# Attention and mixture-of-experts layer on one core: first layers three experts ahead, two bank sets, and the routing weights prepared in two parts

## The chip, the cores and the metric

The kernel runs on one core of one Trainium2 chip, as one launch. The metric is the device time of an execution in microseconds (us); a kernel's time is the median of its runs. Engines: PE is TensorE (PEld its weight loads), DVE is VectorE, ACT is ScalarE, POOL is GpSimd, SP is SyncE, which here only issues transfers.

## The reference

`x` has shape (16, 512, 128) in float32. Two sub-layers follow each other, each added to its input:

```python
x = x + attention(layernorm(x))      # 16 heads of 8, softmax over 512, relative keys and values
n = layernorm(x)                     # second sub-layer, per token
shared = (gelu(n @ sw1 + sb1) @ sw2 + sb2).sum(experts) / 2          # 2 shared experts
gates = n @ router_w + router_b                                      # 8 experts
topv, topi = top_k(gates, 2); probs = softmax(topv)
comb = sum_k one_hot(topi) * probs                                   # (tokens, 8)
y = gelu(n @ w1 + b1) @ w2 + b2                                      # all 8 experts, hidden width 256
x = x + shared + (comb * y).sum(experts)
```

All ten experts are computed for every token; `comb` weighs their results.

## The kernel before

The first 1612 us are attention, in 8 pairs of batches. The change lies in the part behind it, the experts' part: 16 batches of 512 tokens, each with ten experts (two shared, eight routed). The tokens of a batch lie on the free axis of `h_hi` and `h_lo`, the float16 high and low halves of the normalised rows, so a float32 product is made of three float16 ones.

**One expert.** PE's `up` makes the first layer: two halves of the hidden width, each three matmuls with 512 columns, into banks 4 and 5 of PSUM. ACT's `hidden` takes each half through the gelu into `hid` (two instructions, L692), then copies both to float16, `hid_h` (L698). POOL's `low_rows` subtracts (L545): `hid_l = hid - hid_h`, both operands and the result in SBUF. PE's `down` makes the second layer: 24 matmuls with 128 columns, into bank 6 for even experts and bank 7 for odd ones. DVE's `expert` adds the result into `acc`, weighed by `comb` (four instructions, L1025), and raises `y_used`. In the trace `hid` is called probs, `hid_h` and `hid_l` are called probs_t, and `acc`, `h_hi` and `h_lo` are called keys, since they lie in those buffers.

**The order on PE** is written out by hand in `batch`. With LOOK = 2, the step of expert e issues `up(e + 2)` and then `down(e)`; the last two steps issue the first layers of the next batch's experts 0 and 1. Between the steps the next batch is prepared: attention's remainder after step 0 (`prepare_attention`), the output projection after step 1, the transposes of the normalised rows after step 4 (`prepare_h`), the gates after step 5. The routing weights of the batch itself are transposed after step 0 (`prepare_comb`), and after step 2 they are multiplied with the second biases (`second_biases`). These use banks 0 to 3.

**What `down` waits for.** It needs `hid_l` of its expert, and its bank must be free: for experts 2 to 9 that `y_used` of expert e - 2 has come, for experts 0 and 1 that the last expert of the batch before is added (`final_ready`). So `down(9)` waits for DVE to have added expert 7.

**The next batch on DVE.** DVE works in program order: after expert 1 it makes the residual and the statistics, after expert 4 `h_lo`, after expert 5 the gates, the two best of the eight (`gap` is the difference of the two) and `pick`, their one-hot rows. POOL raises e to the power `gap` (`gate_exponentials`, L539, after its subtraction for expert 7), and DVE makes the softmax of two and the weighted `pick`, after expert 7 (L1004 to L1012).

**Loops.** Batches 0 to 13 run in a hardware loop of 7 iterations with two batches each; batches 14 and 15 are written out behind it. Each iteration begins with a load of ACT's function table.

Of the kernel before, what the change touches and what calls it, by code (L numbers as in the profile page):

```python
# [17 lines left out]
P = 128  # L18
# [43 lines left out]
LOOK = 2  # L62
# [12 lines left out]
OWN = {(0, 1): "values0", (1, 0): "values1"}  # L75

# [9 lines left out]
def attention_ffn(nc, x, w_qkv, cols, rows, wo_t, bo, rk_win, rv_win, rw, rb, w1, w2, b2,  # L86
                  sw1, sw2, sb2, b1_cols, consts, rel_scratch, out):
    with ExitStack() as ctx:
# [106 lines left out]
        comb_t = sb("comb_t", [EXPERTS, L])  # L195
# [6 lines left out]
        hid = probs[:, 0:4, :].rearrange("p (e k) c -> p e k c", e=2)  # L202
# [39 lines left out]
        SETUP_POOL = 4  # L242
# [181 lines left out]
        def _(pool):  # L424
# [3 lines left out]
            nc.gpsimd.memset(comb[:], 1.0 / NS / W_SCALE).then_inc(setup_pool, 1)  # L428
            pool.wait_ge(setup_pool, SETUP_POOL)
# [111 lines left out]
            def low_rows(b, slot, e):  # L541

                pool.wait_ge(hid_high, START + b * EXPERTS + e + 1)
                n = slot * EXPERTS + e
                nc.gpsimd.tensor_tensor(hid_l[:, n % SLOTS, :, :], hid[:, n % 2, :, :], hid_h[:, n % SLOTS, :, :],  # L545
                                        ALU.subtract).then_inc(hid_low, 1)
# [19 lines left out]
        def _(act):  # L566
# [118 lines left out]
            def hidden(b, slot, e):  # L685
                n = slot * EXPERTS + e

                act.wait_ge(hid_low, SLOTS + b * EXPERTS + e - 1)
                for k in range(2):

                    act.wait_ge(up_done, START + b * 20 + e * 2 + k + 1)
                    nc.scalar.activation(hid[:, n % 2, k, :], ps[:, 4 + k, :], ACT.Gelu, bias=b1_s[:, e, k:k + 1],  # L692
# [5 lines left out]
                nc.scalar.activation(hid_h[:, n % SLOTS, :, :], hid[:, n % 2, :, :], ACT.Copy).then_inc(hid_high, 1)  # L698

            def batch(b, slot, ahead):  # L700
                for e in range(EXPERTS):
                    hidden(b, slot, e)
                    if e == 2:
                        prepare_weights(b)
                    if ahead and e == 5:
                        normalised(b + 1, 1 - slot)
                    if ahead and e == 6:
                        prepare_h(b + 1, 1 - slot)

            def prepare_weights(b):  # L710

                act.wait_ge(comb_tr, START + b + 1)
                nc.scalar.activation(comb_t[:], ps[0:EXPERTS, 2, :], ACT.Copy).then_inc(comb_t_ready, 1)
# [34 lines left out]
        def _(dve):  # L748
# [164 lines left out]
            def last_step(pair, parity):  # L913
# [16 lines left out]
                rel_out(pair, s)  # L930
                prepare_comb(0, 0, link)
# [12 lines left out]
            FFN_LINKS = 14  # L944
# [36 lines left out]
            def prepare_gates(b, link):  # L981

                dve.wait_ge(gate_done, START + b + 1)
                link(nc.vector.tensor_tensor(gates[:], ps[:, 2, 0:TPB * NE].rearrange("p (t e) -> p t e", t=TPB),
# [16 lines left out]
            def prepare_comb(b, slot, link):  # L1001
# [8 lines left out]
                link(nc.vector.tensor_tensor(pick[:], pick[:], prob2[:].unsqueeze(3).broadcast_to([P, TPB, 2, NE]), ALU.mult))  # L1010
                link.wait()
                nc.vector.tensor_tensor(comb[:, slot, :, NS:], pick[:, :, 0, :], pick[:, :, 1, :], ALU.add).then_inc(comb_ready, 1)  # L1012

            def second_biases(b, slot):

                dve.wait_ge(bias_done, START + b + 1)
                nc.vector.tensor_tensor(acc[:, slot, :, :], ps[:, 3, :].rearrange("p (t d) -> p t d", t=TPB),
                                        acc[:, slot, :, :], ALU.add).then_inc(bias_added, 1)
# [75 lines left out]
            nc.vector.tensor_scalar(b2_s[:], b2_s[:], W_SCALE, None, ALU.mult).then_inc(w_low, 1)  # L1094
# [10 lines left out]
        def _(pe):  # L1105
# [276 lines left out]

            def prepare_attention(b, parity, pair):
# [5 lines left out]


                pe.wait_ge(x1_var, START + b)
# [20 lines left out]
            def prepare_gates(b, slot):  # L1412

                pe.wait_ge(h_ready, START + 2 * b + 1)
                for t in range(TPB):
                    last = nc.tensor.matmul(ps[:, 2, t * NE:(t + 1) * NE], h_t[:, slot, t * P:(t + 1) * P], rw_s[:], start=True, stop=True)
# [9 lines left out]
            def second_biases(b):  # L1426

                pe.wait_ge(comb_t_ready, START + b + 1)
# [155 lines left out]
```

## Time and profile before

| what | value |
|---|---|
| median of 3 runs | 2149.46 us (2146.33 to 2150.55) |
| the profiled execution's own time | 2150.59 us |
| its span, first to last instruction | 2147.1 us |
| PE busy | 2082.1 us, 97% of the span |
| DVE, ACT, POOL busy | 76%, 70%, 54% of the span |
| PE's share of the chain that ended last | 84% |
| TensorE's granted clock over the span | 0.992 |

The span leaves out some 3.5 us around the first and the last instruction. The profiled execution is 1.1 us above the median. In rows of the timeline a matmul's duration is longer than the distance to the next one, since matmuls overlap: what an instruction costs PE is the distance between starts.

### The profile page before, as it was taken

What the parts mean: (1) busy time and instruction counts of PE and PEld (TensorE: products, weight loads), DVE (VectorE), ACT (ScalarE), POOL (GpSimd) and SP (SyncE); (2) the same over time, 40 slices, a digit from 0 to 9 for tenths busy, and PEclk for the clock granted to TensorE, in tenths of its full rate; (3) what the DMA queues carried; (4) which work ended last, traced back from release to release, by engine and by line L of the source; (5) the groups of instructions that cost most, each with busy time, mean ns of one, the idle gap of its engine ahead of it and who ended that gap; (6) DMA issues with size and microseconds to landing.
All of it is one profiled execution on the core that took longest, in us unless ns stands there. A gap on an engine that the chain in (4) does not pass through costs nothing.

```text
span 2147.1 us, 88171 instructions
## 1 busy us (share of the span) xinstructions
PE 2082.1 (97%) x37442; PEld 1544.8 (72%) x37442; DVE 1637.8 (76%) x3856; ACT 1513.3 (70%) x3304; POOL 1161.0 (54%) x1104
## 2 busy tenths in 40 slices
PE   3999999999999999999999999999998999999998
PEld 1777777777777777777777777777775777777776
DVE  4787787788778878977887787788875676677675
ACT  3666676666676676767666776766656888888887
POOL 5454546356354644544563455454415677777676
PEclk8999999999999999999999999999999999999999
DMA  5112211321221123123112211222112212212210
GB/s 139 33 55 66 74 55 45 86 65 54 62 79 55 45 66 81 49 59 89 48 53 66 75 55 55 76 62 58 44 55 23 30 20 24 29 20 24 29 20 11
DMA packets 255681, 114.48 MB, mean 53 GB/s; under 512 B 142218, under 2 KB 251156, under 8 KB 255348
## 3 DMA queue, kind: packets, MB, share of 16 engines
q1 hardware_dynamic: 255348, 109.60, 21.0%
q8 instruction: 263, 4.31, 0.8%
q14 instruction: 70, 0.57, 0.1%
HBM read 83.34 MB, written 8.39 MB: 43 GB/s over the span
## 4 chain that ended last, share of the span: by engine, by line
PE 84%; ACT 5%; POOL 4%; issue 3%; SPq 1%; DVE 1%; DMA 1%; ACTq 0%; POOLq 0%; DVEq 0%
PE ps L1276 21%; PE ps L1211 11%; PE ps L1296 10%; PE ps L1306 8%; PE ps L1218 8%; PE ps L1229 7%; POOL probs_t L545 3%; ACT probs L692 2%; PE ps L1458 2%; PE ps L1441 2%; PE ps L1443 2%; PE ps L1442 2%; PE ps L1460 2%; PE ps L1459 2%; PE ps L1314 1%
## 5 line engine op out<-in xcount | busy, mean ns | idle before, releaser
L624 ACT ACTIVATE probs<-ps,neg_max 128x512 f32<-128x512 f32 x1024 | 690.5, 686 | 352.2 <-DVE neg_max L819 352.1
L819 DVE TENSOR_REDUCE neg_max<-ps 128x1 f32<-128x512 f32 x1024 | 635.5, 682 | 151.7 <-PE ps L1218 147.3
L463 POOL TENSOR_TENSOR stat_hi<-q_twice,mask8h 128x1024 f16<-128x1024 f16 x128 | 242.8, 1897 | 659.1 <-PE ps L1218 594.2
L1276 PE MATMUL ps<-const,probs 128*128 128x128 f32 x4096 | 496.4, 274 | 0.7 <-ACT probs L624 0.6
L1276 PEld LDWEIGHTS ps<-const,probs 128*128 128x128 f32 x4096 | 453.4, 141 | 28.9 <-issue 15.5
L824 DVE COPY probs_t<-ps 128x512 f32<-128x512 f32 x512 | 339.5, 683 | 92.1 <-PE ps L1276 89.4
L545 POOL TENSOR_TENSOR probs_t<-probs,probs_t 128x1024 f16<-128x1024 f32 x160 | 340.1, 2134 | 108.8 <-ACT probs_t L698 108.8
L614 ACT ACTIVATE probs_t<-ps 128x512 f32<-128x512 f32 x512 | 278.6, 595 | 135.9 <-PE ps L1276 133.5
L1211 PE MATMUL ps<-keys,stat_hi 128*32 128x512 f16 x4096 | 318.0, 383 | 0.0
L1218 PE MATMUL ps<-rk_split,stat_rel 96*32 96x512 f16 (+2 forms) x4096 | 281.4, 340 | 0.0
L1025 DVE SCALAR_TENSOR_TENSOR keys<-ps,comb,keys 128x128 f32<-128x128 f32 x640 | 179.7, 343 | 128.7 <-PE ps L1460 128.6
L479 POOL TENSOR_TENSOR stat_rel<-q_rel,mask4h 96x1024 f16<-96x1024 f16 x128 | 251.1, 1962 | 41.7 <-PE ps L1218 30.2
L692 ACT ACTIVATE probs<-ps,b_s 128x512 f32<-128x512 f32 x320 | 205.4, 684 | 53.9 <-PE ps L1443 48.9
L1306 PE MATMUL ps<-probs_t,rv_step 128*32 128x128 f32 x6656 | 226.5, 273 | 2.4 <-DMA rv_step<-in_rv_win 2.4
L1458 PE MATMUL ps<-w_h,probs_t 128*128 128x128 f16 x1280 | 222.8, 219 | 5.3 <-DVE keys L1025 1.8
L1296 PE MATMUL ps<-probs_t,v_s 128*32 128x128 f32 x6656 | 226.2, 272 | 0.0
L1460 PE MATMUL ps<-w_h,probs_t 128*128 128x128 f16 x1280 | 222.6, 219 | 0.0
L1459 PE MATMUL ps<-w_l,probs_t 128*128 128x128 f16 x1280 | 222.6, 219 | 0.0
L624 ACT ACTIVATION_READ_ACCUMULATOR probs<-ps,neg_max 128x1 f32 x1024 | 207.4, 203 | 0.0
L1211 PEld LDWEIGHTS ps<-keys,stat_hi 128*32 128x32 f16 x4096 | 91.3, 96 | 158.1 <-issue 108.2
L1296 PEld LDWEIGHTS ps<-probs_t,v_s 128*32 128x32 f32 x6656 | 185.2, 109 | 22.1 <-issue 0.3
L473 POOL TENSOR_TENSOR stat_lo<-q_lo_pair,mask8h 128x128 f16<-128x128 f16 x512 | 191.2, 406 | 0.0
(135 smaller groups left out, 2900.4 us busy)
## 6 DMA issues: line engine op xcount, KB each, us to landing
rv_step<-in_rv_win SPq DMA_DIRECT2D x128, 512.0 KB, 3.9
keys<-keys SPq DMA_DIRECT2D x64, 96.0 KB, 2.7
x_pair<-in_x SPq DMA_DIRECT2D x8, 512.0 KB, 4.6
q_twice<-q_hi SPq DMA_DIRECT2D x32, 128.0 KB, 2.9
q_lo_pair<-q_lo SPq DMA_DIRECT2D x32, 128.0 KB, 2.6
rel_scratch<-rel_t SPq DMA_DIRECT2D x256, 16.0 KB, 3.2
x_pair<-in_x SPq DMA_DIRECT2D x16, 256.0 KB, 3.1
x_pair<-rel_scratch SPq DMA_DIRECT2D x64, 64.0 KB, 3.9
```

The costliest lines, as they stand in the source:

```text
L545: nc.gpsimd.tensor_tensor(hid_l[:, n % SLOTS, :, :], hid[:, n % 2, :, :], hid_h[:, n % SLOTS, :, :], ALU.subtract).then_inc(hid_low, 1)
L614: nc.scalar.activation(probs_t[s % 2][:, q, :, :].rearrange("p r c -> p (r c)"), ps[:, tr_bank(q), :], ACT.Copy).then_inc(evac_act, 1)
L624: nc.scalar.activation(probs[:, q, :], ps[:, i, :], ACT.Exp, bias=neg_max[:, q:q + 1], accum_out=row_sum[parity][:, s * QUADS + q:s * QUAD ...
L819: nc.vector.tensor_reduce(neg_max[:, q:q + 1], ps[:, i, :], op=ALU.max, axis=AX_X, negate=True).then_inc(max_done, 1)
L824: nc.vector.tensor_copy(probs_t[s % 2][:, q, :, :].rearrange("p r c -> p (r c)"), ps[:, tr_bank(q), :]).then_inc(evac_dve, 1)
L1211: nc.tensor.matmul(ps[at:at + 32, q % IN_ROUND, :], stat_hi[s % 2][:, half, b, q, :], group_keys(k_both[parity][:, half, b, :], group), st ...
L1218: last = nc.tensor.matmul(ps[32 * g:32 * g + 32, q % IN_ROUND, L - near:L], stat_rel[s % 2][:, q, g, :, :].rearrange("k l h -> k (l h)"), ...
L1276: last = nc.tensor.transpose(ps[:, bank, rt * P:(rt + 1) * P], probs[:, q, rt * P:(rt + 1) * P], ident)
L1296: nc.tensor.matmul(ps[32 * g:32 * g + 32, AV_BANK, b * P:(b + 1) * P], values[:, 32 * g:32 * g + 32], cols, start=rt == 0, stop=rt == RT - ...
L1306: last = nc.tensor.matmul(ps[32 * g:32 * g + 32, AV_BANK, (2 + half) * P:(3 + half) * P], rv_step[:, RT - 1 - block, q * 32:q * 32 + 32], ...
L1458: nc.tensor.matmul(y, hid_h[:, place, k, rows], w2_h[:, e, k, :], start=k == 0, stop=False)
L1459: nc.tensor.matmul(y, hid_h[:, place, k, rows], w2_l[:, e, k, :], start=False, stop=False)
```

## The change

LOOK becomes 3: a step issues `up(e + 3)` and `down(e)`. First layers of even experts go to banks 4 and 5, those of odd ones to banks 2 and 3 (`up_bank`), and `up` waits for the gelu of the expert two before. `hid` has four places in place of two. All preparation now uses banks 0 and 1. The routing weights are split into float16 parts on DVE (`comb_split`: high, low, high) before PE transposes them, and the second biases too (`b2_split`), so that their product is one float16 matmul per 128 tokens over 96 rows. That product moves to after step 3, the transposes to after step 1. `down(0)` waits for expert 8 of the batch before in place of expert 9. POOL's two powers come later in its order, and DVE's softmax part stands alone as `prepare_choice`, after expert 6.

```diff
-LOOK = 2
+LOOK = 3
+def up_bank(e, k):
+    return (4 if e % 2 == 0 else 2) + k
...
-        hid = probs[:, 0:4, :].rearrange("p (e k) c -> p e k c", e=2)
+        hid = probs[:].rearrange("p (e k) c -> p e k c", e=SLOTS)
...
             def batch(b, slot, ahead):            # POOL
                 for e in range(EXPERTS):
                     low_rows(b, slot, e)
-                    if ahead and e == 3:
+                    if ahead and e == 5:
                         deviations_after(b + 1)
-                    if ahead and e == 7:
+                    if ahead and e == 8:
                         gate_exponentials(b + 1)
...
             def hidden(b, slot, e):               # ACT
-                act.wait_ge(hid_low, SLOTS + b * EXPERTS + e - 1)
+                act.wait_ge(hid_low, SLOTS + b * EXPERTS + e - SLOTS + 1)
...
-                    if e == 2:
+                    if e == 4:
                         prepare_weights(b)
-                    if ahead and e == 5:
+                    if ahead and e == 6:
                         normalised(b + 1, 1 - slot)
-                    if ahead and e == 6:
+                    if ahead and e == 7:
                         prepare_h(b + 1, 1 - slot)
...
-            def prepare_comb(b, slot, link):      # DVE
+            def prepare_choice(b, link):
...
                 link(nc.vector.tensor_tensor(pick[:], pick[:], prob2[:].unsqueeze(3).broadcast_to([P, TPB, 2, NE]), ALU.mult))
+
+            def prepare_comb(b, slot, link):
+
                 link.wait()
-                nc.vector.tensor_tensor(comb[:, slot, :, NS:], pick[:, :, 0, :], pick[:, :, 1, :], ALU.add).then_inc(comb_ready, 1)
+                link(nc.vector.tensor_tensor(comb[:, slot, :, NS:], pick[:, :, 0, :], pick[:, :, 1, :], ALU.add))
+                link.wait()
+
+                dve.wait_ge(comb_tr, START + b)
+                weights = comb[:, slot, :, :]
+                link(nc.vector.tensor_scalar(comb_split[:, :, 0:3:2, 0:EXPERTS], weights.unsqueeze(2).broadcast_to([P, TPB, 2, EXPERTS]),
+                                             W_SCALE, None, ALU.mult))
+                link.wait()
+                nc.vector.scalar_tensor_tensor(comb_split[:, :, 1, 0:EXPERTS], weights, W_SCALE, comb_split[:, :, 0, 0:EXPERTS],
+                                               ALU.mult, ALU.subtract).then_inc(comb_ready, 1)
...
+                        if e == 6:
+                            prepare_choice(b + 1, link)
                         if e == 7:
                             prepare_comb(b + 1, 1 - slot, link)
...
-                    last = nc.tensor.transpose(ps[0:EXPERTS, 2, t * P:(t + 1) * P], comb[:, slot, t, :], ident)
+                    halves_of = comb_split[:, t, :, :].rearrange("p a e -> p (a e)")
+                    last = nc.tensor.transpose(bank_h(0, L)[0:3 * 32, t * P:(t + 1) * P], halves_of, identh[:])
...
-                    last = nc.tensor.matmul(ps[:, 3, t * D:(t + 1) * D], comb_t[:, t * P:(t + 1) * P], b2_s[:], start=True, stop=True)
+                    last = nc.tensor.matmul(ps[:, 1, t * D:(t + 1) * D], comb_t[:, t * P:(t + 1) * P], b2_split[:], start=True, stop=True)
...
-                    pe.wait_ge(gelu_done, START + b * 20 + (e * 2 + k - 1 if e else 0))
+                    if b is not first_batch or e >= 2:
+
+                        pe.wait_ge(gelu_done, START + b * 20 + e * 2 + k - 3)
...
-                if e >= 2:
-                    pe.wait_ge(y_used, START + b * (EXPERTS - 1) + e - 1)
+                if e == 1:
+                    pe.wait_ge(final_ready, START + b)
                 else:
-                    pe.wait_ge(final_ready, START + b)
+                    pe.wait_ge(y_used, START + b * (EXPERTS - 1) + max(e - 1, 0))
...
-                    if e == 0:
+                    if e == 1:
                         prepare_comb(b, slot)
-                    if e == 2:
-                        second_biases(b)
+                    if e == 3:
+                        second_biases(b, ahead)
```

On DVE, in batch 14, where the code is written out, these rows stand between the one-hot rows of the next batch and the second biases. The row of keys<-ps,comb,keys is `expert`, four instructions for each expert, so x8 are experts 6 and 7. In the kernel before:

```order
L996 TENSOR_TENSOR gap<-top 128x4
L998 TENSOR_TENSOR pick<-const,top_f 128x64
L1025 SCALAR_TENSOR_TENSOR keys<-ps,comb,keys 128x128 x8
L1004 TENSOR_SCALAR prob<-e_gap 128x4
L1006 RECIPROCAL prob<-prob 128x4
L1008 TENSOR_TENSOR prob<-prob,e_gap 128x4
L1010 TENSOR_TENSOR pick<-pick,prob 128x64
L1012 TENSOR_TENSOR comb<-pick 128x4x8
```

And in the changed kernel, at the same place:

```order
L1008 TENSOR_TENSOR gap<-top 128x4
L1010 TENSOR_TENSOR pick<-const,top_f 128x64
L1049 SCALAR_TENSOR_TENSOR keys<-ps,comb,keys 128x128 x4
L1016 TENSOR_SCALAR prob<-e_gap 128x4
L1018 RECIPROCAL prob<-prob 128x4
L1020 TENSOR_TENSOR prob<-prob,e_gap 128x4
L1022 TENSOR_TENSOR pick<-pick,prob 128x64
L1049 SCALAR_TENSOR_TENSOR keys<-ps,comb,keys 128x128 x4
L1027 TENSOR_TENSOR comb<-pick 128x4x8
L1032 TENSOR_SCALAR comb_split<-comb 128x4x2x10
L1035 SCALAR_TENSOR_TENSOR comb_split<-comb,comb_split 128x4x10
```

Four of the five steps of the softmax part now stand ahead of expert 7, and two new instructions follow the fifth.

On POOL, in the same batch, the row of probs_t is the subtraction for one expert. In the kernel before:

```order
L545 TENSOR_TENSOR probs_t<-probs,probs_t 128x1024 [waits hid_high] x4
L532 TENSOR_TENSOR rstd<-var_eps,half_pow 128x4 [waits x1_var]
L534 TENSOR_TENSOR shift<-neg_mean,rstd 128x4 [waits pool_link]
L545 TENSOR_TENSOR probs_t<-probs,probs_t 128x1024 [waits hid_high] x4
L539 TENSOR_TENSOR e_gap<-e_const,gap 128x4 [waits gap_ready]
L545 TENSOR_TENSOR probs_t<-probs,probs_t 128x1024 [waits hid_high] x12
```

And in the changed kernel:

```order
L555 TENSOR_TENSOR probs_t<-probs,probs_t 128x1024 [waits hid_high] x6
L542 TENSOR_TENSOR rstd<-var_eps,half_pow 128x4 [waits x1_var]
L544 TENSOR_TENSOR shift<-neg_mean,rstd 128x4 [waits pool_link]
L555 TENSOR_TENSOR probs_t<-probs,probs_t 128x1024 [waits hid_high] x3
L549 TENSOR_TENSOR e_gap<-e_const,gap 128x4 [waits gap_ready]
L555 TENSOR_TENSOR probs_t<-probs,probs_t 128x1024 [waits hid_high] x11
```

The first power moved behind two more subtractions, the second behind one more. Behind the second, the rest of the batch's experts and all of batch 15 follow.

## Rows read from the trace of the kernel before

**Rows 1.** The page's first part: busy us, share of the span and instructions.
```profile
PE 2082.1 (97%) x37442; PEld 1544.8 (72%) x37442; DVE 1637.8 (76%) x3856; ACT 1513.3 (70%) x3304; POOL 1161.0 (54%) x1104
```

**Rows 2.** Timeline of ACT: start us, us, engine, line, operation, tiles, count, idle before.
```profile
1689.50 1.28 ACT L692 ACT_TABLE_LOAD   x1 [0.85 <-POOL probs_t L545]
...
1754.18 1.28 ACT L692 ACT_TABLE_LOAD   x1 [0.85 <-POOL probs_t L545]
...
1767.80 1.34 ACT L692 ACTIVATE probs<-ps,b_s 128x512 f32<-128x512 f32 x2 [1.10 <-PE ps L1443]
1769.23 1.06 ACT L698 ACTIVATE probs_t<-probs 128x1024 f16<-128x1024 f32 x1
...
1774.02 1.63 ACT L676 ACTIVATE q_f<-keys,shift,rstd 128x128 f32<-128x128 f32 x4
```

**Rows 3.** Timeline of PE over parts of one batch.
```profile
1757.52 0.22 PE L1458 MATMUL ps<-w_h,probs_t 128*128 128x128 f16 x1
...
1758.86 0.38 PE L1441 MATMUL ps<-keys,w_h 128*128 128x512 f16 x1
...
1761.60 0.60 PE L1387 MATMUL ps<-const,x_pair 128*128 128x128 f32 x4
...
1762.93 0.60 PE L1423 MATMUL ps<-const,comb 128*10 128x128 f32 x4
1763.37 0.38 PE L1441 MATMUL ps<-keys,w_h 128*128 128x512 f16 x1
...
1766.01 1.11 PE L1402 MATMUL ps<-wo_s,xn_t 128*128 128x128 f32 x8
1766.95 0.38 PE L1441 MATMUL ps<-keys,w_h 128*128 128x512 f16 x1
...
1769.68 1.15 PE L1430 MATMUL ps<-b_s,comb_t 10*128 10x128 f32 x8
1770.77 0.39 PE L1441 MATMUL ps<-keys,w_h 128*128 128x512 f16 x1
```

**Rows 4.** Timeline of POOL and DVE around the softmax part of a loop batch.
```profile
1750.97 1.01 POOL L539 TENSOR_TENSOR e_gap<-e_const,gap 128x4 f32<-128x4 f32 x1 [0.17 <-DVE gap L996]
1751.95 4.22 POOL L545 TENSOR_TENSOR probs_t<-probs,probs_t 128x1024 f16<-128x1024 f32 x2
...
1754.40 1.78 DVE L1008 TENSOR_TENSOR prob<-prob,e_gap 128x4 f32<-128x4 f32 x1
```

**Rows 5.** Timeline of POOL, DVE and PE, the same part in batch 14.
```profile
2107.36 4.22 POOL L545 TENSOR_TENSOR probs_t<-probs,probs_t 128x1024 f16<-128x1024 f32 x2
2112.01 2.14 POOL L545 TENSOR_TENSOR probs_t<-probs,probs_t 128x1024 f16<-128x1024 f32 x1 [0.43 <-ACT probs_t L698]
...
2109.46 2.14 DVE L1004 TENSOR_SCALAR prob<-e_gap 128x4 f32<-128x4 f32 x1
...
2111.85 0.16 DVE L1008 TENSOR_TENSOR prob<-prob,e_gap 128x4 f32<-128x4 f32 x1
2112.05 2.18 DVE L1010 TENSOR_TENSOR pick<-pick,prob 128x64 f32<-128x64 f32 x1
...
2114.37 2.28 DVE L1025 SCALAR_TENSOR_TENSOR keys<-ps,comb,keys 128x128 f32<-128x128 f32 x8
...
2116.80 0.22 PE L1458 MATMUL ps<-w_h,probs_t 128*128 128x128 f16 x1 [1.81 <-DVE keys L1025]
```

**Rows 6.** Timeline of DVE between the low half and the choice of experts.
```profile
1778.95 0.69 DVE L979 TENSOR_TENSOR keys<-ps,keys 128x512 f16<-128x512 f32 x1 [1.58 <-ACT keys L683]
...
1782.03 1.43 DVE L995 CAST top_f<-top_i 128x8 f32<-128x8 uint32 x1
```

**Rows 7.** PE's longest waits: before the first batch, with the clock, and at the end.
```profile
1616.69 0.69 PE L1409 MATMUL ps<-const,q_f 128*128 128x128 f32 x2 [4.29 <-ACT q_f L676]
...
1616.00:1620.00 4.00, 2.63 (x12) 2.23 (x13) 0.69 (x1) 2.78 (x5) 0.00 (x0) 0.50 0.00 0
...
2141.16 0.23 PE L1458 MATMUL ps<-w_h,probs_t 128*128 128x128 f16 x1 [1.12 <-POOL probs_t L545]
```

More of the change, by code:

```diff
@@ L544, in low_rows @@
                 n = slot * EXPERTS + e
-                nc.gpsimd.tensor_tensor(hid_l[:, n % SLOTS, :, :], hid[:, n % 2, :, :], hid_h[:, n % SLOTS, :, :],
+                nc.gpsimd.tensor_tensor(hid_l[:, n % SLOTS, :, :], hid[:, n % SLOTS, :, :], hid_h[:, n % SLOTS, :, :],
                                         ALU.subtract).then_inc(hid_low, 1)
@@ L686, in hidden @@
                 n = slot * EXPERTS + e
-                act.wait_ge(hid_low, SLOTS + b * EXPERTS + e - 1)
+                act.wait_ge(hid_low, SLOTS + b * EXPERTS + e - SLOTS + 1)
                 for k in range(2):
                     act.wait_ge(up_done, START + b * 20 + e * 2 + k + 1)
-                    nc.scalar.activation(hid[:, n % 2, k, :], ps[:, 4 + k, :], ACT.Gelu, bias=b1_s[:, e, k:k + 1],
+                    nc.scalar.activation(hid[:, n % SLOTS, k, :], ps[:, up_bank(e, k), :], ACT.Gelu, bias=b1_s[:, e, k:k + 1],
                                          scale=1.0 / W_SCALE).then_inc(gelu_done, 1)
@@ L697, in hidden @@
                 act.wait_ge(gelu_done, START + b * 20 + e * 2 + 2)
-                nc.scalar.activation(hid_h[:, n % SLOTS, :, :], hid[:, n % 2, :, :], ACT.Copy).then_inc(hid_high, 1)
+                nc.scalar.activation(hid_h[:, n % SLOTS, :, :], hid[:, n % SLOTS, :, :], ACT.Copy).then_inc(hid_high, 1)
             def batch(b, slot, ahead):
@@ L712, in prepare_weights @@
                 act.wait_ge(comb_tr, START + b + 1)
-                nc.scalar.activation(comb_t[:], ps[0:EXPERTS, 2, :], ACT.Copy).then_inc(comb_t_ready, 1)
+                nc.scalar.activation(comb_t[:], bank_h(0, L)[0:3 * 32, :], ACT.Copy).then_inc(comb_t_ready, 1)
             for half in range(2):
@@ L1093, in _ @@
             dve.wait_ge(ffn_loaded, 16 * FFN_LOADS)
-            nc.vector.tensor_scalar(b2_s[:], b2_s[:], W_SCALE, None, ALU.mult).then_inc(w_low, 1)
+            for row in (0, 1):
+                nc.vector.tensor_scalar(b2_split[32 * row:32 * row + EXPERTS, :], b2_s[:], W_SCALE, None, ALU.mult).then_inc(w_low, 1)
+            dve.wait_ge(w_low, 4)
+            nc.vector.scalar_tensor_tensor(b2_split[64:64 + EXPERTS, :], b2_s[:], W_SCALE, b2_split[0:EXPERTS, :], ALU.mult, ALU.subtract).then_inc(w_low, 1)
             pair_steps(PAIRS - 1, 1, False, False)
@@ L1388, in prepare_attention @@
                 last.then_inc(rel_nat_tr, 1)
-                pe.wait_ge(x1_var, START + b)
+                if b is not first_batch:
+                    pe.wait_ge(gap_ready, START + b)
                 for l in range(QT):
@@ L1412, in prepare_gates @@
             def prepare_gates(b, slot):
+                pe.wait_ge(bias_added, START + b)
                 pe.wait_ge(h_ready, START + 2 * b + 1)
                 for t in range(TPB):
-                    last = nc.tensor.matmul(ps[:, 2, t * NE:(t + 1) * NE], h_t[:, slot, t * P:(t + 1) * P], rw_s[:], start=True, stop=True)
+                    last = nc.tensor.matmul(ps[:, 1, t * NE:(t + 1) * NE], h_t[:, slot, t * P:(t + 1) * P], rw_s[:], start=True, stop=True)
                 last.then_inc(gate_done, 1)
```

30 lines of the change are left out of this document (19 added, 11 removed).

## The prediction, made before the changed kernel ran

> **What bounds the kernel now.** The page comes first: PE is busy for 97% of the span, and nothing else comes near [rows 1]. So the change is worth what it takes from PE's work or from its waits, in the experts' part alone, since attention is left as it is. The length of a batch is read from ACT's timeline: the table load at the top of each loop iteration comes every 64.68 us [rows 2], so a batch takes 32.34 us.
>
> What PE works in it is read from distances between starts [rows 3]. A second layer takes 1.34 us (1757.52 to 1758.86), both layers 2.64 (1763.37 to 1766.01), so a first layer 1.30. Attention's remainder takes 1.33, four float32 transposes 0.44, the output projection 0.94. The second biases begin after a second layer that ends at 1766.95 + 2.64 = 1769.59, and the next first layer starts at 1770.77: 1.18. With another set of transposes (0.44) and the gates, eight passes as the projection (0.94), a batch is 26.4 + 1.33 + 0.44 + 0.94 + 1.18 + 0.44 + 0.94 = 31.67 us of work. So PE waits only 0.67 us per batch: that, and what becomes cheaper, is all there is to win.
>
> The third thing to see is DVE against POOL. The multiply L1008, of 4 columns, takes 0.16 us when POOL is idle [rows 5], but 1.78 when asked for at 1754.40, while POOL's second subtraction runs; it ends at 1756.18, with that subtraction (1751.95 + 4.22 = 1756.17) [rows 4]. In batch 14 L1004 takes 2.14 and L1010 2.18 in the same way, behind the subtractions that end at 2111.58 and 2114.15 [rows 5]. A small DVE instruction on SBUF operands that is asked for while POOL subtracts is held until POOL's instruction is over, up to 2.1 us. Expert 7 and its neighbours read their matmul result from PSUM and don't show this: eight take 2.28 [rows 5]. In batch 14 the held steps made PE wait 1.81 us for DVE, in front of a second layer [rows 5].
>
> **What becomes cheaper.** The second biases become four float16 matmuls with 128 columns. A second layer has 24 such in 1.34 us, so 0.056 each and 0.25 with a little for the start: 0.93 less. The transposes of the weights become float16, four by 0.056: 0.22 less. Work is then 31.67 - 1.15 = 30.52. Bounds: were they as slow as float32 ones, nothing is won; 1.18 and 0.44 are the most. I take the float16 rate, the same shape as in a row. The split of b2 is four small instructions, once, under attention's PE work: nothing, and 2 us each if that cover failed and POOL held them. Four places for `hid` and two bank sets let ACT go on without POOL, and the table load's 1.28 us, behind which PE waited, finds cover. I take the 0.67 us of waits as gone. ACT needs 2.40 us for an expert (1.34 + 1.06, [rows 2]), under PE's 2.64, so it doesn't become the bound.
>
> **A timetable of one batch**, from the start of `up(3)` at 0, all engines caught up. First layers start at 0, 4.0 (1.33 for attention's remainder), 7.8 (0.94 and 0.22), 10.4, and 13.3 (0.25 for the biases). A first layer's copy is finished 0.85 + 1.43 + 1.06 = 3.34 us after its start (1766.95 to 1767.80, 1769.23, and 1.06) [rows 2, 3].
> - The power for the next batch's rows now stands behind POOL's subtraction for expert 5. That one starts at 7.8 + 3.4 = 11.2 and ends at 13.3; the power (1.01, [rows 4]) and the product with the mean end at 14.6, ACT's normalisation (1.63, [rows 2]) at 16.25. PE asks for it at 15.95: a new wait of 0.4 us. A batch without other waits is 30.9 us. Further first layers: 16.8, 20.4 (behind the gates), 23.0, 25.6, 28.3; `down(9)` could start at 29.6.
> - ACT, late by the normalisation, copies expert 7 by 18.6, the rows of the next batch (two copies, about 1 us) by 19.6, experts 8, 9 and the next batch's 0 and 1 by 21.9, 24.3, 26.7 and 29.1.
> - DVE's low half starts at 19.6, and the cast of the indices 3.1 us behind (1778.95 to 1782.03, [rows 6]), at 22.7. POOL subtracts for expert 8 from 22.0 to 24.1, so the cast is held until then, as now. Then `gap`, and POOL's power from 24.25 to 25.25.
> - POOL then has work in store, since PE and ACT run three experts ahead: it subtracts for 9 from 25.2, for 0 from 27.35, for 1 from 29.5 to 31.6, and the inputs (24.3, 26.7, 29.1) are there each time.
> - DVE adds expert 6 from 24.3 to 25.4. The softmax part, which stood behind expert 7, is next, each step waiting for the one before. L1004 is asked for at 25.4 and held to 27.4, L1008 at 27.6 and held to 29.5, L1010 at 29.6 and held to 31.7. Expert 7 ends at 32.9 (1.14, half of 2.28, [rows 5]), and `down(9)`, which needs its bank, starts at 33.05 instead of 29.6: 3.5 us of PE waiting. Behind DVE's held steps expert 7 is queued, and behind it PE's next steps with the next batch's first layers.
>
> So such a batch takes 34.4 us, 2.06 more than now; there are nine of them (transitions into batches without a table load). Before the other six, ACT loads its table, so the copy of the next batch's expert 0 comes at 28.0, POOL is idle from 27.35, and L1008 and L1010 slip through at 27.6 to 28.05: expert 7 is in time. Then the sum and the two new split steps meet POOL's subtractions again; one more held step puts expert 8 at about 33.7, and `down(0)` asks at 30.9 + 1.3 = 32.2: 1.6 us. These take 32.5, 0.2 more. Each new step costs 0.2 (as L1008's 0.16) free and 2.2 (as L1010's) held; with both split steps held it is 3.8 us and not 1.6.
>
> On both inputs in SBUF the Trainium skill (SBUF — State Buffer, SBUF: two separate sides) says that VectorE and GpSimd share one pair of ports under an exclusive lock: a VectorE instruction with two SBUF inputs, or a single-source one in a two-port mode, and a GpSimd one block each other for the whole instruction. By that rule both split steps can be held, and the biases' addition, with one input in PSUM, can't; rows 4 and 5 agree for the four instructions that they show, and none shows a split step. The sum takes one held step of the three; by the rule alone all three could be.
>
> **The sum.** Nine by 2.06 is 18.5, six by 0.2 is 1.2. Less: batch 14's 1.8 us, now counted as an ordinary batch; 1.15 of cheaper work in batch 15; about 1.0 of the 1.12 us that PE waits for POOL at the last second layer [rows 7], since its first layer is a step earlier; and up to 1.3, one first layer done while the part fills, taken whole. 18.5 + 1.2 - 5.25 = +14.5. The profiled execution's 2150.6 (span 2147.1 and 3.5 around it) becomes 2165; it is 1.1 above the median, so 2164 to 2165. I take 2165.
>
> **The rivals.**
> - *The steps don't line up with POOL* (the other side). If at most one of the three is held, expert 7 ends before 29.6, and PE doesn't wait. A batch is 30.9: 15 x -1.44 - 5.25 = -27, that is 2124. For it: in the loop batches now only one step is clearly held. Against it: now ACT must wait for POOL after two experts, which leaves POOL idle when L1010 comes; the change takes just that away. It decides at 0.6 to 0.9 us, the margins by which the inputs are ahead of POOL.
> - *Two of three held*: expert 7 ends at 30.9, PE waits 1.4, batches stay at 32.3: about 2147, 2140 to 2155.
> - *TensorE's clock falls in the new waits.* After 4.29 us of waiting it was granted 0.50, half of 2.4 GHz, from 1616 to 1620 [rows 7]; 1.81 us left it whole. 3.5 lies nearer to the first. If a step of 2.64 us then ran at half rate, nine by 2.64 is 24 more: 2189. That idling lowers this clock is also what the Trainium skill says (TensorE: Matmul & The Clock Gate, Part 1: The HAM clock gate); the rows agree.
> - *Both split steps held* before the six loads: 6 x 2.2 = 13 more, 2178.
>
> **Chances.** Three held (2158 to 2182, with the split steps' case): 0.52. Clock falls as well (2180 to 2205): 0.10. Two held: 0.18. None or one: 0.17. Something else: 0.03. Of 2149.5, 0.2% is 4.3 us, about what a measurement can tell from no change. Faster gets 0.17 + 0.07, the same 0.08, slower 0.68. The range for 8 in 10 takes in two held and part of the clock's case, 2134 to 2190; the likeliest case's own is 2158 to 2182.
>
> **What would show it.** L1008 and L1010 (now L1020, L1022) at 2 us each in most loop batches; PE waiting 3 to 4 us for DVE before a second layer once a batch, and 0.4 us for ACT before the transposes; the second biases at 0.25 us; table loads 67 us apart. I am wrong if POOL shows idle time between the subtractions behind its second power, or if the table loads are 62 us apart.

## The result, and the profile after

The changed kernel takes 2174.03 us (median of 4 runs, 2171.59 to 2176.66), the kernel before beside it 2147.94 (4 runs): 1.0121 times as long, 95% interval 1.0101 to 1.0140. That is 26 us slower; the forecast was 2165, 15.5 slower. The profiled execution is the shortest of the four (2171.59, span 2169.8). In lines of waits, the three numbers are us in total, times, and the longest.

The first part of the page, the row that answers to [rows 1]:

```profile
PE 2076.6 (96%) x37378; PEld 1540.4 (71%) x37378; DVE 1726.4 (80%) x3890; ACT 1514.1 (70%) x3304; POOL 1161.1 (54%) x1106
```

DVE has 89 us more busy time than before with 34 more instructions: it is held. POOL's work is what it was. ACT's table loads, against [rows 2]:

```profile
1755.16 1.28 ACT L703 ACT_TABLE_LOAD   x1
...
1823.37 1.28 ACT L703 ACT_TABLE_LOAD   x1
```

They are 68.21 us apart, where the kernel before had 64.68. Two batches cost 3.5 us more. Between the two profiled executions the spans differ by 22.7 us: the five pairs of batches between the second load and the last (1687.01 to 2028.10, before 1689.50 to 2012.87) are 17.7 longer, what stands behind the last load 7.5 longer, and what stands ahead of the second 2.5 shorter. So the loss is in the batches, most of it in the loop. The waits there, from 1650 to 2110 us:

```profile
PE ps L1499 <- DVE keys L1049: 31.3, 14, 3.0
...
ACT q_f L686 <- POOL shift L544: 14.6, 13, 1.3
...
PE ps L1468 <- DVE var_eps L986: 4.1, 13, 0.5
```

The first line is two waits, `down(9)`'s and `down(0)`'s; the other two belong to the statistics of the next rows. First the softmax part, in a transition without a table load. Timeline of DVE, POOL, ACT and PE, to be laid beside [rows 4]:

```profile
1788.85 1.94 DVE L1016 TENSOR_SCALAR prob<-e_gap 128x4 f32<-128x4 f32 x1
...
1791.04 1.83 DVE L1020 TENSOR_TENSOR prob<-prob,e_gap 128x4 f32<-128x4 f32 x1
1792.91 2.11 DVE L1022 TENSOR_TENSOR pick<-pick,prob 128x64 f32<-128x64 f32 x1
1794.94 1.11 DVE L1049 SCALAR_TENSOR_TENSOR keys<-ps,comb,keys 128x128 f32<-128x128 f32 x4
...
1787.66 1.01 POOL L549 TENSOR_TENSOR e_gap<-e_const,gap 128x4 f32<-128x4 f32 x1 [0.17 <-DVE gap L1008]
1788.64 8.55 POOL L555 TENSOR_TENSOR probs_t<-probs,probs_t 128x1024 f16<-128x1024 f32 x4
...
1791.30 1.06 ACT L709 ACTIVATE probs_t<-probs 128x1024 f16<-128x1024 f32 x1
...
1796.11 0.29 PE L1499 MATMUL ps<-w_h,probs_t 128*128 128x128 f16 x1 [3.00 <-DVE keys L1049]
```

POOL runs four subtractions in a row (8.55 us). L1016, L1020 and L1022 each end with one of them, and cost 5.88 us where 0.6 would do. Expert 7, which reads its matmul results from PSUM, starts at once when they are through; `down(9)` has waited 3.00 us. This is the forecast's picture, to a few tenths.

The window behind that wait (busy time by engine, then the granted clock, as in [rows 7]):

```profile
1796.00:1800.00 4.00, 3.89 (x29) 3.14 (x30) 3.67 (x12) 0.23 (x1) 1.19 (x1) 0.60 0.00 0
```

Behind the wait the granted clock is 0.60 on average over 4 us: part of them at full speed, 2.4 GHz, and part at half. `down(9)` takes 2.53 us instead of 1.34 (starts of its first matmul and of the next first layer's), and the first layer 1.58 instead of 1.30: 1.5 us. Nine transitions have a wait of 3.0 us, and seven of them such a fall; the kernel before has a granted clock of 1.00 from 1630 us to its end.

The second place is `down(0)`, in the transitions with a table load. L1020 and L1022 take 0.17 and 0.22 us there, and a split step is held (DVE, POOL, PE):

```profile
1761.40 2.04 DVE L1035 SCALAR_TENSOR_TENSOR comb_split<-comb,comb_split 128x40 f16<-128x40 f32 x1
...
1761.25 2.13 POOL L555 TENSOR_TENSOR probs_t<-probs,probs_t 128x1024 f16<-128x1024 f32 x1 [0.17 <-ACT probs_t L709]
...
1764.53 0.23 PE L1499 MATMUL ps<-w_h,probs_t 128*128 128x128 f16 x1 [1.22 <-DVE keys L1049]
```

The third place is earlier in the batch, at the statistics of the next rows (DVE, POOL, ACT, PE):

```profile
1774.67 1.93 DVE L985 TENSOR_SCALAR neg_mean<-mv 128x4 f32<-128x4 f32 x1
...
1774.43 2.13 POOL L555 TENSOR_TENSOR probs_t<-probs,probs_t 128x1024 f16<-128x1024 f32 x1 [1.67 <-ACT probs_t L709]
1776.74 1.01 POOL L542 TENSOR_TENSOR rstd<-var_eps,half_pow 128x4 f32<-128x4 f32 x1 [0.18 <-DVE var_eps L986]
...
1778.06 1.26 ACT L686 ACTIVATE q_f<-keys,shift,rstd 128x128 f32<-128x128 f32 x3 [1.07 <-POOL shift L544]
...
1776.72 0.34 PE L1468 MATMUL ps<-b_split,comb_t 96*128 96x128 f16 x3 [0.27 <-DVE var_eps L986]
```

The negated mean (L985), a step that the prediction didn't speak of, is held 1.93 us by the subtraction for expert 5, which now stands ahead of the power. The variance (L986) comes behind it and raises `x1_var`, for which the changed `second_biases` waits before it writes bank 1 (a line of the change that its diff above leaves out); so the bias matmuls wait 0.27 us, and ACT's normalisation 1.07 us for POOL. What that last wait does is seen only in experiment 10.

### The profile page after: what moved, and what is told of

Same layout as the page of the kernel before. It is cut to its first block, busy times and chain, and to the rows that moved or that the text cites. A ratio compares the mean times of both kernels' runs of the same rounds, so it can differ in the third digit from the quotient of the medians.

```text
span 2169.8 us, 88111 instructions
## 1 busy us (share of the span) xinstructions
PE 2076.6 (96%) x37378; PEld 1540.4 (71%) x37378; DVE 1726.4 (80%) x3890; ACT 1514.1 (70%) x3304; POOL 1161.1 (54%) x1106
## 4 chain that ended last, share of the span: by engine, by line
PE 77%; DVE 10%; issue 6%; ACT 3%; POOL 2%; SPq 1%; DMA 1%; DVEq 0%; ACTq 0%; POOLq 0%
PE ps L1305 21%; PE ps L1240 11%; PE ps L1325 10%; PE ps L1335 8%; PE ps L1247 8%; PE ps L1258 6%; DVE keys L1049 3%; DVE prob L1016 1%; PE ps L1499 1%; PE ps L1343 1%; PE ps L1501 1%; PE ps L1500 1%; ACT q_f L686 1%; DVE prob L1020 1%; DVE keys L975 1%
## 5 line engine op out<-in xcount | busy, mean ns | idle before, releaser
L1499 PE MATMUL ps<-w_h,probs_t 128*128 128x128 f16 x1280 | 229.5, 223 | 34.4 <-DVE keys L1049 34.4
L1500 PE MATMUL ps<-w_l,probs_t 128*128 128x128 f16 x1280 | 229.6, 223 | 0.0
L1501 PE MATMUL ps<-w_h,probs_t 128*128 128x128 f16 x1280 | 229.6, 223 | 0.0
```

The lines of the kernel that those rows point to most:

```text
L1500: nc.tensor.matmul(y, hid_h[:, place, k, rows], w2_l[:, e, k, :], start=False, stop=False)
L1501: last = nc.tensor.matmul(y, hid_l[:, place, k, rows], w2_h[:, e, k, :], start=False, stop=k == 1)
```

## The experiments

Each ratio is against runs of the kernel before that were taken beside it; their medians are 2148.49 us for runs 1 to 4, 2148.72 for 5 to 8 and 2147.78 for 9 to 12. Line numbers are of each run's own kernel, and shift by up to 20. A "pair" is two batches, from one table load of ACT to the next.

**1. The choice behind expert 7 again.**

```diff
-                        if e == 6:
-                            prepare_choice(b + 1, link)
                         if e == 7:
+                            prepare_choice(b + 1, link)
                             prepare_comb(b + 1, 1 - slot, link)
```

> The changed kernel with prepare_choice moved back behind expert 7, directly ahead of prepare_comb, as before the change. Held-steps theory: down(9) no longer waits, but the same steps, and the three of prepare_comb, now meet POOL's subtractions in front of expert 8, so the wait of about 3 us moves to down(0) of the next batch: 2160 to 2180 us. Rival (the early place in front of expert 7 alone is the cause, since before it stood behind expert 7): the waits vanish, 2120 to 2130 us.

2172.86 us, ratio 1.0113 (1.0095 to 1.0131): no change against the changed kernel. Three steps are held, but others (L1020, L1022, and the first split step), and the wait is `down(0)`'s. DVE and PE:

```profile
1795.43 1.84 DVE L1020 TENSOR_TENSOR prob<-prob,e_gap 128x4 f32<-128x4 f32 x1
1797.30 2.12 DVE L1022 TENSOR_TENSOR pick<-pick,prob 128x64 f32<-128x64 f32 x1
...
1799.69 2.01 DVE L1032 TENSOR_SCALAR comb_split<-comb 128x80 f16<-128x80 f32 x1
...
1803.03 0.29 PE L1498 MATMUL ps<-w_h,probs_t 128*128 128x128 f16 x1 [2.89 <-DVE keys L1049]
```

So the place of the choice isn't the cause in the changed kernel; that three of the steps are held, wherever they stand, is.

**2. The steps as reciprocals.** L1016, L1020 and L1022 become reciprocals of 128x4, as L1018 is. The softmax's values, the weights of the experts and so the output are no longer the reference's.

```diff
-                link(nc.vector.tensor_tensor(prob2[:, :, 1], prob2[:, :, 0], e_gap[:], ALU.mult))
+                link(nc.vector.reciprocal(prob2[:, :, 1], prob2[:, :, 0]))
```

> The four steps of the softmax part stay where they are, as a chain of four dependent instructions, but each is a reciprocal of 128x4 with a single input, which was never held in the traces (0.18 us each, POOL busy or not); the weights are therefore not the softmax. Held-steps theory: down(9) doesn't wait any more, the clock doesn't fall, and only prepare_comb's three steps are held behind expert 7: 2122 to 2140 us. Rival (the chain of semaphore waits and its place delay expert 7, whatever the instructions): as the changed kernel, 2170 to 2178 us.

2132.98 us, ratio 0.9928 (0.9912 to 0.9943), as the held-steps theory had it. DVE, with POOL subtracting from 1782.98 to 1789.29:

```profile
1783.19 0.18 DVE L1016 RECIPROCAL prob<-e_gap 128x4 f32<-128x4 f32 x1
...
1783.62 0.18 DVE L1020 RECIPROCAL prob<-prob 128x4 f32<-128x4 f32 x1
1783.83 0.18 DVE L1022 RECIPROCAL prob<-prob 128x4 f32<-128x4 f32 x1
...
1785.18 2.08 DVE L1027 TENSOR_TENSOR comb<-pick 128x32 f32<-128x32 f32 x1
1787.29 2.07 DVE L1032 TENSOR_SCALAR comb_split<-comb 128x80 f16<-128x80 f32 x1
```

Not one reciprocal is held, though POOL subtracts and their operands lie in SBUF as those of the held steps do; the sum and the split step behind them are. Against the changed kernel the held steps are worth 41 us, more than the whole loss.

**3. A look-ahead of two.** `LOOK = 2` in the changed kernel, all else left.

> The changed kernel with LOOK = 2 and nothing else. Held-steps theory: with first layers only two ahead, the input of POOL's subtraction for the next batch's expert 0 comes 1.5 us or more after POOL is free, so at most one or two of the three steps are held: wait before down(9) under 1 us, 2125 to 2145 us. Rival (looking ahead saves PE waits and has nothing to do with the loss): slower than the changed kernel by the waits of before that come back, 2174 to 2190 us.

2253.75 us, ratio 1.0495 (1.0478 to 1.0513): both missed. The orders of ACT and POOL are written out for a look-ahead of three, and PE now waits for ACT too:

```profile
PE ps L1441 <- ACT q_f L686: 29.1, 11, 2.9
```

It tells nothing of the look-ahead, since it changed more than that; run 9 asks the question rightly.

**4. One step for each expert.** The sum with the power and its reciprocal (L1016, L1018) behind expert 6, L1020 behind 7, L1022 behind 8, `prepare_comb` behind 9.

```diff
                         if e == 7:
+                            prepare_second(link)
+                        if e == 8:
+                            prepare_weighted(link)
+                        if e == 9:
                             prepare_comb(b + 1, 1 - slot, link)
```

> The same instructions, spread: power's sum and reciprocal behind expert 6, the product behind expert 7, the weighted pick behind expert 8, prepare_comb behind expert 9. Held-steps theory: each held step costs up to 2.1 us, but DVE has 2.6 us between the end of an expert's sum and the second layer that needs its bank, so PE doesn't wait for it: a batch of about 31 us, no fall of the clock, 2115 to 2130 us, faster than the kernel before. Rival (DVE as a whole is the bound, 80% busy in the page): the wait only moves, 2160 us or more.

2141.22 us, ratio 0.9959 (0.9946 to 0.9973): in the theory's direction, its size missed by 11 us. `down(9)` and `down(0)` no longer wait, but the split step behind expert 9, held 2.0 us in every second batch, puts attention's addition late:

```profile
PE ps L1446 <- DVE xn_t L967: 13.1, 6, 2.2
```

**5. The early place alone, in the kernel before.**

```diff
+                        if e == 6:
+                            prepare_choice(b + 1, link)
                         if e == 7:
                             prepare_comb(b + 1, 1 - slot, link)
```

> The kernel before, with the choice in a part of its own and that part alone moved from behind expert 7 to behind expert 6; look-ahead, banks and biases as before. Held-steps theory: what makes the place costly is that POOL has subtractions in store, and with first layers two ahead it has none when the fourth step comes; one step or two are held (2 us each) as in the kernel before, and DVE's expert 7 has 2.6 us more to wait for: 2148 to 2156 us, the kernel before within its noise or up to 0.35% above it, no fall of the clock in the loop. Rival, the place alone is the cause: three steps held here too, waits of 3 us before down(9), 2165 to 2180.

2164.61 us, ratio 1.0068 (1.0055 to 1.0082): between the two, and both missed. Two steps are held, not one, and the third finds POOL idle; the pair is 66.32, against 64.68. DVE, then POOL:

```profile
1792.16 1.94 DVE L1005 TENSOR_SCALAR prob<-e_gap 128x4 f32<-128x4 f32 x1
...
1794.36 1.84 DVE L1009 TENSOR_TENSOR prob<-prob,e_gap 128x4 f32<-128x4 f32 x1
1796.23 0.22 DVE L1011 TENSOR_TENSOR pick<-pick,prob 128x64 f32<-128x64 f32 x1
...
1791.95 4.22 POOL L545 TENSOR_TENSOR probs_t<-probs,probs_t 128x1024 f16<-128x1024 f32 x2
1796.69 2.13 POOL L545 TENSOR_TENSOR probs_t<-probs,probs_t 128x1024 f16<-128x1024 f32 x1 [0.52 <-ACT probs_t L698]
```

PE waits 0.5 to 1.0 us for it, in 15 places. The early place is dear by itself, 16 us.

**6. The float16 second biases alone, in the kernel before** (the split, the transposes, the matmuls and the addition's scale, as in the change's diff, in banks 2 and 3).

> The kernel before, with the float16 second biases and their split alone; look-ahead of two and the choice in one part, as before. The bias matmuls at 0.25 us instead of 1.18 and the transposes of the weights at 0.22 instead of 0.44 take 1.15 us per batch from PE: 16 x 1.15 = 18 us, 2130, if none of it comes back as waiting. Held-steps theory: the split steps come last in a chain already held once, so each one held (2 us) in half of the batches puts the bank of expert 8 late by about 1 us: 2130 to 2148. Rival, the biases carry the loss of the full change (the two split steps): 2155 to 2175.

2150.23 us, ratio 1.0009 (1.0000 to 1.0018), pair 64.78: just outside the theory's 2130 to 2148 and short of the rival's 2155. The 1.15 us of work per batch is won and waited for again: 1.82 us for DVE once a pair, where the sum is held 2.01, and 0.72 us for POOL in each batch (14 in the loop). That the look-ahead of two leaves PE too near to POOL is my reading; no run was made for it.

**7. The clock kept up.** Eight matmuls whose result nobody uses, in the wait ahead of `down(9)`, in every second batch.

```diff
+                    if ahead and slot == 0 and e == EXPERTS - 1:
+                        for k in range(8):
+                            nc.tensor.matmul(ps[:, 0, :], w1_h[:, 0, 0:P], h_hi[:, slot, :], start=True, stop=True)
```

> The changed kernel with eight extra float16 matmuls of 512 columns (1.7 us in all, their result unused) into a bank that is free, directly ahead of down(9) in every second batch, where PE waits 3.0 us for DVE. They fill half of the wait and leave 1.3 us of it. Theory that the clock's falls cost 1.5 us each (down(9) 2.57 instead of 1.34, the next first layer 1.58 instead of 1.30): no falls there, table loads 66.9 instead of 68.2 us apart, 2164 (2160 to 2168). Rival, what is lost at the lower clock would have been waited for anyhow: 2171 to 2177, the table loads 68.2 apart.

2165.05 us, ratio 1.0074 (1.0060 to 1.0087): 9 us less than the changed kernel, with more work. (In the expectation, 2.57 should read 2.53.) PE, then the window behind the wait:

```profile
1796.94 1.89 PE L1512 MATMUL ps<-keys,w_h 128*128 128x512 f16 x8
1800.11 0.23 PE L1499 MATMUL ps<-w_h,probs_t 128*128 128x128 f16 x1 [1.28 <-DVE keys L1049]
...
1800.00:1804.00 4.00, 3.89 (x52) 3.06 (x53) 3.67 (x12) 1.60 (x3) 1.18 (x1) 1.00 0.00 0
```

`down(9)` starts no earlier after expert 7, but at the full clock, and the pair is 66.79. A fall costs 1.4 us. Eight of the nine waits are filled, among them all seven that had a fall in the changed kernel, and none of the eight has one now. The ninth, of 2.99 us at the end of the loop, isn't filled; a fall follows it here, which it didn't in the changed kernel. So there are six falls fewer, and 9 us are 1.5 for each.

**8. Spread steps, the split in the batch itself, the power earlier.** Run 4, with `comb_split` made behind the batch's own expert 0, and POOL's first power behind its subtraction for expert 4. (What the expectation calls row maximum and comparison are the sum with the power and its reciprocal.)

```diff
-                    if ahead and e == 5:
+                    if ahead and e == 4:
                         deviations_after(b + 1)
...
+                    if e == 0:
+                        split_weights(b, slot, link)
```

> The changed kernel with the softmax part spread as in the fourth run (row maximum and comparison behind expert 6, the product behind 7, the gap's product behind 8, the sum behind 9), the two split steps moved on to the batch itself behind its own expert 0, and POOL's power for the next rows behind its subtraction for expert 4 instead of 5. Held-steps theory: at most one step is held ahead of any expert, expert 9 is ahead of xn_t's addition by itself, the product with the mean ends 2 us earlier, so the waits of 2.18, 0.35 and 0.23 us of the fourth run go: a batch at 30.6 to 31.0 us, 2115 to 2127. Rival, the held steps only move their wait on to the next consumer (the biases, which need the split 2.6 us sooner after it): 2135 to 2145, with PE waiting for the weights' transposes.

2115.74 us, ratio 0.9847 (0.9833 to 0.9860), the shortest time of all, 33 us under the kernel before. In the loop PE has one wait of 0.5 us left; the pair is 60.77, so a batch's own work is 30.39 us (the prediction worked out 30.52). Steps are still held (L1018 1.94, others 0.7 to 1.4), one ahead of each expert, and no one waits for them.

**9. The look-ahead alone.** The changed kernel with float32 second biases, without split steps, the choice behind expert 7: three ahead, two sets of banks and the later powers remain.

> The changed kernel with its look-ahead of three, its bank sets and its later powers alone: the second biases are float32 again, without split steps, and the choice stands behind expert 7 in one piece, as in the kernel before. Theory that the look-ahead is what brings the held steps: POOL has subtractions in store behind its power, so three steps are held one behind the other, with PE's work at 31.5 us and a wait of 2 to 3 us in every second batch: 2150 to 2170, more than the kernel before. Rival, the look-ahead by itself only takes away the 0.67 us of waits per batch and the loss needs the moved choice or the split: 2135 to 2142.

2141.09 us, ratio 0.9969 (0.9958 to 0.9980): the rival's 2135 to 2142, and not my 2150 to 2170. Three ahead is a small gain by itself. POOL runs only two subtractions without a gap behind its power; from the third on it waits for ACT's input, 0.21 and then 0.50 us (DVE, then POOL):

```profile
1789.37 2.09 DVE L1016 TENSOR_TENSOR prob<-prob,e_gap 128x4 f32<-128x4 f32 x1
1791.48 0.22 DVE L1018 TENSOR_TENSOR pick<-pick,prob 128x64 f32<-128x64 f32 x1
...
1789.30 2.13 POOL L551 TENSOR_TENSOR probs_t<-probs,probs_t 128x1024 f16<-128x1024 f32 x1 [0.21 <-ACT probs_t L705]
1791.93 2.13 POOL L551 TENSOR_TENSOR probs_t<-probs,probs_t 128x1024 f16<-128x1024 f32 x1 [0.50 <-ACT probs_t L705]
```

Two steps are held and the third takes 0.22 us. This kernel differs from run 1's only in the second biases and their split, and run 1 takes 2172.86 us: with the look-ahead of three and the later powers in place, the float16 biases cost some 31 us (run 1 is 24 above its kernel before, this one 7 below).

**10. POOL's first power one expert earlier**, and nothing else.

```diff
-                    if ahead and e == 5:
+                    if ahead and e == 4:
                         deviations_after(b + 1)
```

> The changed kernel with POOL's power for the next batch's rows behind its subtraction for expert 4 instead of expert 5, and nothing else. Theory: the product with the mean is no longer held (2.0 us) and the wait of 0.3 us (0.43 to 0.52 of lost time with its start) before the bias matmuls and that of 0.17 before the transposes of h go, in each of 15 batches; the waits for DVE before down(9) and down(0) stay: 2174 less 15 x 0.6 = 2165 (2162 to 2170). Rival, the time won there is waited for again at down(9), since POOL's order of subtractions sets it: 2171 to 2177.

2127.23 us, ratio 0.9901 (0.9886 to 0.9916): 47 us less than the changed kernel from one number, where I expected 9. (The "product with the mean" of the expectation is the negated mean, L985.) POOL now stands at the power and waits there for DVE, so nothing holds L985:

```profile
1798.56 0.17 DVE L985 TENSOR_SCALAR neg_mean<-mv 128x4 f32<-128x4 f32 x1
...
1798.88 1.01 POOL L542 TENSOR_TENSOR rstd<-var_eps,half_pow 128x4 f32<-128x4 f32 x1 [2.23 <-DVE var_eps L986]
```

ACT's 1.07 us of waiting is gone (L686 follows without a pause), and that reaches as far as the softmax part, three experts on. DVE, POOL, ACT and PE there:

```profile
1782.59 1.84 DVE L1020 TENSOR_TENSOR prob<-prob,e_gap 128x4 f32<-128x4 f32 x1
1784.47 0.22 DVE L1022 TENSOR_TENSOR pick<-pick,prob 128x64 f32<-128x64 f32 x1
...
1779.21 1.01 POOL L549 TENSOR_TENSOR e_gap<-e_const,gap 128x4 f32<-128x4 f32 x1 [0.17 <-DVE gap L1008]
1780.19 4.22 POOL L555 TENSOR_TENSOR probs_t<-probs,probs_t 128x1024 f16<-128x1024 f32 x2
...
1784.51 2.17 POOL L555 TENSOR_TENSOR probs_t<-probs,probs_t 128x1024 f16<-128x1024 f32 x1
...
1783.38 1.06 ACT L709 ACTIVATE probs_t<-probs 128x1024 f16<-128x1024 f32 x1
...
1778.47 0.38 PE L1481 MATMUL ps<-keys,w_h 128*128 128x512 f16 x1
...
1785.79 0.23 PE L1499 MATMUL ps<-w_h,probs_t 128*128 128x128 f16 x1 [0.59 <-DVE keys L1049]
```

ACT hands over the third input at 1784.44, just after POOL's second subtraction ends (1780.19 + 4.22 = 1784.41). The third starts at 1784.51, a gap of 0.10 us, and L1022, at 1784.47, slips into it. In the changed kernel ACT had the third input ready at 1792.36 (1791.30 + 1.06), half a microsecond before POOL came to it, so there was no gap. One held step less takes `down(9)`'s wait from 3.00 to 0.59 us, and with it the clock's fall.

What is late in the changed kernel at this place is POOL, and not ACT. In both kernels ACT begins on the first layer that feeds the third subtraction 0.85 us after PE does (1789.02 to 1789.87 there, 1781.10 to 1781.95 here). But POOL's power starts 0.74 us after a first layer here (1778.47 to 1779.21), and 1.27 in the changed kernel, where that layer's first row is:

```profile
1786.39 0.38 PE L1481 MATMUL ps<-keys,w_h 128*128 128x512 f16 x1
```

The half microsecond comes from the normalisation. Two copies on, ACT is still 0.53 us later against PE than here (its copy ends 1.10 us ahead of a first layer and not 1.63), and with it come later POOL's subtraction, which holds DVE's cast of the indices (L1007), and `gap` and the power behind that. ACT then catches up with PE, and POOL doesn't. The distance from first layer to power is 1.27 us in run 1 too (1790.78 to 1792.05), where three steps are held, and 0.64 in run 9 (1783.25 to 1783.89), where two are.

**11. Run 8 with the power left behind expert 5.**

> The fourth run's spread with the two split steps moved into the batch itself behind its expert 0, POOL's power left behind expert 5. Theory: the 2.18 us wait before the output projection goes (once in two batches), the waits before the biases and h stay (0.6 us in each batch): 2116 + 15 x 0.6 = 2125 (2121 to 2130). Rival, the power's place is what mattered in the eighth run: 2134 to 2142, as the fourth run.

2126.69 us, ratio 0.9900 (0.9885 to 0.9915), as expected. The wait before the output projection is gone; that for `var_eps` remains (4.4 us in 14 places). The power's place alone, the one difference from run 8, is worth 11 us in this order.

**12. Run 8 with float32 second biases.**

> The eighth run's kernel with the second biases in float32 again, without split steps. Theory that PE alone sets the length of a batch there (30.39 us): the biases cost their whole 1.15 us, 16 x 1.15 = 18: 2134 (2131 to 2137). Rival, the split steps that fall away give something back by way of fewer held steps: 2125 to 2130.

2132.58 us, ratio 0.9936 (0.9922 to 0.9950), as expected: 17 us more than run 8, near the full price of the float32 biases (16 by 1.15 is 18), where PE has no other wait.

## Why the prediction was near, and where its sum was off

The direction, the mechanism and the place were right, and run 2 shows them: take the held steps away and the kernel is 41 us shorter. The changed kernel's loss isn't the sum of its parts: the early choice alone gave +16 (run 5), the biases +1.5 (run 6) and the look-ahead with the later powers -7 us (run 9), together 11, and the whole 26.

Point by point, for a pair of 66.9 us forecast and 68.2 measured:
- **Cheaper work**, 30.52 us a batch: 30.39 in run 8. Right, and run 12 shows the 1.15 us as 17 in all.
- **Nine transitions with three held steps**, 3.5 us at `down(9)`: 3.00 of idle time (it starts 3.16 us later than it could). Right; the steps were held 1.83 to 2.11 us, and expert 7 took 1.11.
- **Six with one held split step**, 1.6 us at `down(0)`: the wait is 1.22 us (`down(0)` starts 1.39 later than it could) and L1035 is held 2.04. Right. By the Trainium skill's rule (SBUF — State Buffer, SBUF: two separate sides) both split steps can be held, and across runs both were: L1035 here, L1032 in run 1 (2.01).
- **0.4 us of new waiting for ACT** before the transposes of `h`: 0.17. The missing part is ahead of it, at the bias matmuls, 0.43 to 0.52 us lost per batch for `var_eps`. The step that failed here is "That one starts at 7.8 + 3.4 = 11.2 and ends at 13.3; the power (1.01, [rows 4]) and the product with the mean end at 14.6": I let POOL's subtraction for expert 5 delay only POOL's own power. I left out that it holds DVE's L985 for the same time (1.93 us), and that the bias matmuls now wait for the variance behind it.
- **TensorE's clock in the new waits**, a rival with 10%: this is the term that the sum lacked. It fell after seven of the nine waits of 3.0 us, at 1.5 us each and not the 2.64 that the rival reckoned: 10 us, and run 7, which has six falls fewer, gave 9 back.

Worked out again with these, a pair is 60.78 of work, 3.16 and 1.39 at the second layers, 1.5 for the clock, 0.95 at the biases and 0.34 at the transposes: 68.1. So two terms were missing, 2.45 us together, and four were 1.3 us too large together; that the sum came within 9 us of the median (and 6.6 of the profiled execution, for which 2165 was worked out) is in part luck.

The rival on the other side, that the steps don't line up, was to decide at 0.6 to 0.9 us, the time by which the inputs are ahead of POOL. In the changed kernel the third input is 0.56 us ahead, and run 10 passed that point. It has two steps held and a wait of 0.6 us; the rival of two held steps reckoned 1.4 for it, and a time 20 us longer than run 10's.

So the look-ahead alone isn't what makes the change slow (run 9). It is slow because the first power stands behind one subtraction too many: ACT comes late out of its normalisation, POOL's second power starts late by that, and POOL then finds its next three inputs ready and holds three steps in a row. The two ends of this chain, the power's place and the time, are shown by run 10, the links between them by rows alone. The float16 biases are needed too (run 1 against run 9, some 31 us). That PE has 1.15 us less to do in each batch with them, and so gives ACT no time to catch up before the power, fits the rows of run 9; but they bring the split steps as well, and no run parts the two.

## What to carry to other kernels

Where one engine's large operations hold another's small instructions, count the small steps that stand in a row between two large ones: one held step hides behind a 2.6 us stage, three don't, so spread a dependent chain with one link to a stage. An engine that stands waiting at its own next small step is quiet, and lets the other's pass; a large operation moved ahead of it for more overlap is what holds them. And price a wait on TensorE of 2 to 3 us with its clock's fall: unused matmuls in eight waits gave 9 us back here.

## What was not expected of the hardware

- A reciprocal of 128x4 on DVE takes 0.18 us while POOL subtracts, where a multiply or a scaling of the same size and place takes up to 2.1 (run 2, four in a row). The rule of the Trainium skill (SBUF — State Buffer, SBUF: two separate sides) names instructions with two SBUF inputs and those in a two-port mode. A reciprocal that isn't held agrees with it; a scaling with one input (L1016, L985, L1032) that is held agrees if it runs in such a mode, which no run here shows.
- A held DVE step doesn't block POOL's next one: four subtractions follow one another without a pause (8.55 us) while DVE gets one step in at each boundary, and its successor, asked for 0.04 us later, is held again.
- The clock fell after seven of nine waits of 3.0 us, and not after 1.82 (run 6) or 1.28 (run 7). At 2.18 it went both ways: of run 4's six waits for `xn_t`, the third and the sixth were followed by a fall (at 1831 and 2026 us). The third's pair took 65.87 us instead of 64.36; the sixth is in the last pair, which no table load ends. Windows around the two, granted clock 0.80 and 0.67:

```profile
1826.00:1834.00 8.00, 5.82 (x46) 4.55 (x46) 6.36 (x13) 2.83 (x5) 4.25 (x2) 0.80 0.09 28
2024.00:2028.00 4.00, 2.40 (x13) 2.39 (x14) 2.53 (x7) 0.00 (x0) 2.12 (x1) 0.67 0.00 0
```
